# Two of ScalarE's stages change slots: the copy of the first block's transposed attention, and its tiny exponential

## The reference

```
# block 0, channel attention with a squeeze gate
energy = einsum('bcn,bdn->bcd', q, q)                       # q = x as (b, 128, 256)
attention = softmax(max(energy, -1) - energy)
out = einsum('bcd,bdn->bcn', attention, q)
h = relu(concat([x, out], 1).mean((2, 3)) @ w1.T + b1)
se = sigmoid(h @ w2.T + b2)
x = se * x + (1 - se) * out
```

## Time and profile before

| what | value |
|---|---|
| median of 3 runs | 554.14 us |
| lowest and highest | 550.01 and 558.89 us |
| the profiled execution | 552.4 us |
| its span, first to last instruction | 550.6 us |
| granted TensorE clock, mean | 0.922 of 2.4 GHz |
| TensorE busy | 470.5 us, 85% |
| VectorE busy | 348.1 us, 63% |
| ScalarE busy | 262.7 us, 48% |
| GpSimd busy | 134.0 us, 24% |

### The profile page before, as it was taken

How to read it: one execution, slowest core, us unless ns; L and a number is a source line. 1 busy time by engine, 2 the same in 40 slices (tenths; PEclk the granted TensorE clock), 3 DMA queues, 4 the chain that set the end, 5 groups by cost and what they waited for, 6 DMA issues and landing times.

```text
span 550.6 us, 10106 instructions
## 1 busy us (share of the span) xinstructions
PE 470.5 (85%) x3522; PEld 363.9 (66%) x3522; DVE 348.1 (63%) x895; ACT 262.7 (48%) x654; POOL 134.0 (24%) x161
## 2 busy tenths in 40 slices
PE   4286797879998999899889989999998999884995
PEld 3163564556776768676767766676766788784885
DVE  1418844872868577556867775776538343666896
ACT  3332665743554464435454635533444431994541
POOL 5210563242103102110220022111101111512672
PEclk9997786967999999699999989996998899996999
DMA  6000111000000000000000000000000000004112
GB/s 208 19 19 2 43 44 63 0 21 19 2 1 21 20 1 19 19 0 0 19 19 0 0 19 0 0 20 2 1 1 19 2 20 1 2 1 152 40 38 76
DMA packets 9486, 13.15 MB, mean 24 GB/s; under 512 B 496, under 2 KB 8816, under 8 KB 9328
## 3 DMA queue, kind: packets, MB, share of 16 engines
q1 hardware_dynamic: 9456, 12.76, 7.0%
HBM read 8.56 MB, written 4.19 MB: 23 GB/s over the span
## 4 chain that ended last, share of the span: by engine, by line
PE 57%; DVE 17%; ACT 10%; issue 8%; POOL 4%; DMA 4%; DVEq 0%; SPq 0%; ACTq 0%; POOLq 0%
PE bank L1199 7%; PE bank L1201 5%; PE bank L1200 5%; PE bank L1312 5%; PE bank L1394 5%; PE bank L1368 4%; DMA w_stage<-convs 4%; PE bank L1366 2%; PE bank L1344 2%; PE bank L1422 2%; PE bank L1228 2%; ACT x L798 2%; PE bank L1381 2%; ACT prob L740 1%; DVE even L892 1%
## 5 line engine op out<-in xcount | busy, mean ns | idle before, releaser
L1199 PE MATMUL bank<-win,w_hi 128*128 128x256 f32 x384 | 122.3, 318 | 12.3 <-DVE win L1145 5.9
L740 ACT ACTIVATE prob<-bank 128x512 f32<-128x512 f32 x128 | 69.5, 596 | 95.4 <-PE bank L1366 94.7
L1200 PE MATMUL bank<-win,w_hi 128*128 128x256 f32 x384 | 109.4, 285 | 0.0
L1201 PE MATMUL bank<-win,w_lo 128*128 128x256 f32 x384 | 109.3, 285 | 0.0
L992 DVE TENSOR_REDUCE nmax<-bank 128x2 f32<-128x512 f32 x128 | 85.3, 685 | 34.3 <-PE bank L1344 33.9
L1199 PEld LDWEIGHTS bank<-win,w_hi 128*128 128x128 f32 x384 | 74.0, 193 | 23.7 <-issue 10.8
L1200 PEld LDWEIGHTS bank<-win,w_hi 128*128 128x128 f32 x384 | 74.1, 193 | 0.7
L1201 PEld LDWEIGHTS bank<-win,w_lo 128*128 128x128 f32 x384 | 73.7, 192 | 0.0
L517 POOL TENSOR_TENSOR first<-first 128x256 f32<-128x256 f32 x24 | 17.7, 737 | 174.6 <-ACT first L629 174.6
L1368 PE MATMUL bank<-qk 32*128 32x256 f32 x256 | 43.9, 357 | 4.3 <-ACT prob L740 3.8
L1368 PEld LDWEIGHTS bank<-qk 32*128 32x128 f32 x256 | 26.4, 204 | 19.6 <-issue 6.9
(11 more groups left out here) (235 smaller groups left out, 930.4 us busy)
## 6 DMA issues: line engine op xcount, KB each, us to landing
w_stage<-convs SPq DMA_DIRECT2D x4, 576.0 KB, 4.8
x_in<-x SPq DMA_DIRECT2D x8, 256.0 KB, 2.6
out<-x_pair SPq DMA_DIRECT2D x8, 256.0 KB, 2.2
q<-out SPq DMA_DIRECT2D x1, 2048.0 KB, 8.3
out<-v SPq DMA_DIRECT2D x8, 256.0 KB, 2.1
cst<-small SPq DMA_DIRECT2D x1, 1708.0 KB, 9.7
cst<-small SPq DMA_DIRECT2D x1, 253.5 KB, 2.9
```

Of the source, the lines that this page charges most:

```text
L740: act.activation(prob[:, x // 4 % 2, x % 4, :, :], bank[ST_BANK[x % 2]][:, :], ACT.Exp, scale=L2_SCALE).then_inc(st_exp, 1)
L1199: mm(dst, hi, x_hi, start=(row == 0), stop=False)
L1200: mm(dst, hi, x_lo, start=False, stop=False)
L1201: return mm(dst, lo, x_hi, start=False, stop=(row == KH - 1))
```

## The change

Two entries of ScalarE's table get another slot. "att0t" goes from slot 8 to slot 7, and stands there ahead of "ab" in the order of the table; "z0" goes from slot 15 to slot 14. The stages' own code, waits and semaphores stay, as do the tables of the other engines.

```
-ACT_SLOTS = {"xr": 0, "xt": 2, "sum_x": 3, "hid1": 3, "z1": 4, "att0": 6, "ab": 7, "att0t": 8, "o0": 11, "even": 11, "att1": 11,
-             "hid0": 13, "filt": 13, "z0": 15, "red": 19}
+ACT_SLOTS = {"xr": 0, "xt": 2, "sum_x": 3, "hid1": 3, "z1": 4, "att0": 6, "att0t": 7, "ab": 7, "o0": 11, "even": 11, "att1": 11,
+             "hid0": 13, "filt": 13, "z0": 14, "red": 19}
```

## The result

The changed kernel takes 531.33 us (median of 4 runs, 526.66 to 537.17) against 555.03 us for the kernel before (4 runs, 550.01 to 558.89). The ratio is 0.9595, with a 95% interval of 0.9535 to 0.9654: faster by 4.1%. The profiled execution took 526.66 us, span 524.9 us; it is 25.7 us shorter than that of before, and 0.954 of the full clock was granted over its span where before had 0.922.

The account below looks back on a forecast made before the run. TensorE, 57% of the chain of waits, was taken to bind. Copy 7.0, exponential 4.65 and clock 2.3 us sum to 13.95, say 13.9 us: 540.2 us on the median's scale, 2.5% faster; range 533.5 to 548.0 us.

Parts of the forecast that it names:

- The copy, by order of work: ScalarE's copy (line 649) in slot 7 ends TensorE's wait at line 1228: 7.0 us, low end 4.2, high end 8.7.
- new wait at line 1274: At full clock, with the copy's stall gone, TensorE would wait some 0.8 us for VectorE's logits.
- "ab" and GpSimd's sign product have cover: ScalarE's "ab" would start 0.6 us later, but GpSimd's sign product would keep 2.5 us of slack, costing nothing.
- Round 0's 1.0 us: In round 0 GpSimd's sign product ends at 70.16 regardless, so line 1270 moves from 71.22 to about 70.2, 1.0 us.
- The exponential, by order of work: z0 in slot 14 ends TensorE's wait at line 1291 in rounds 1 to 5: 4.65 us, low end 0.
- The sum of the two: A full-clock round, line 1228 to line 1228, shortens from 49.4 us by 1.7 to 47.7 us.
- The clock: TensorE's drops to 1.2 GHz in rounds 0, 3 and 5 may go: 4.6 us, low end 0, half taken, 2.3.
- rival A: The clock gives back all its 4.6 us: 16.2 us in total, 537.9 us; chance 0.20.
- B: VectorE takes the stall back; the copy yields its low end, the clock nothing: 8.9 us, 545.2 us; chance 0.20.
- C: The copy's stall only moves to line 1274 or the next score products; z0 alone pays: 4.65 us, 549.5 us; chance 0.10.
- D: Slower than before, above 554 us: idle time at line 1274 and elsewhere drops the clock in full-clock rounds; chance 0.05.

## Why the prediction was wrong

By its own steps:

- **The copy, by order of work.** Right in mechanism. At full clock I took 0.8 us a round; measured 1.01 (49.41 to 48.40 with the copy alone). In all that is some 5 us and not 7.0: I booked the whole stall, 1.44 and 1.5 us, for the rounds at half clock, but after the change rounds 2 to 5 run at full clock, where a new wait at line 1274 takes part of it back. The new wait at line 1274 was forecast at some 0.8 us and is 0.69 us, VectorE's queue is what makes it, and the 0.28 us at line 1279 went as said. The claim that "ab" and GpSimd's sign product have cover holds, 2.6 us against 2.5. Round 0's 1.0 us did not come, for a load landed later; that it was booked on one profile's date for the load was the mistake.
- **The exponential, by order of work.** Right: 0.93 us forecast and 1.0 us measured, in rounds 1 to 5, with none in round 0.
- **The sum of the two.** 47.7 us was forecast for a round at full clock; it takes 47.4.
- **The clock.** This is the term that failed. I named the mechanism, TensorE falling to 1.2 GHz in the stall, but sized it at 2.3 us with 4.6 us as its most. It is 14.9 us in the rounds of the profile, and 10.7 to 16 us by the two kernels in which the copy's stall, alone or with the other, is filled. Two mistakes made it small. First, I counted only drops that start in the stall itself or within 1 us behind it (rounds 0, 3 and 5; the one of round 3 begins at 222.5, when line 1228 already runs). Round 1's long drop starts earlier, at 113.3, behind a wait of 1.23 us at line 1223, and I let it stand; yet with the copy's stall gone it was shorter, and the round went from 0.88 to 0.97 of the clock, which is worth 6.63 - 2.0 = 4.6 us. I left out the drop in round 6 too, for its round has none of the moved stages. It cost 4.3 us all the same: from line 1291 of round 5 to that of round 6 before takes 50.27 us and the changed kernel 46.00. Second, I halved the term because a shorter stall remains at line 1274, and put its low end at 0 because rounds 2 and 4 had the same stall and no drop. The remaining stall, 0.69 us, brought no drop in rounds 2 to 5 of the changed kernel. And rounds 2 and 4 say that a stall doesn't bring a drop each time, not that a drop seen had another cause; the kernels with the copy's stall filled show no drop in rounds 2 to 5 at all.
- **The rule of the Trainium skill** (TensorE: Matmul & The Clock Gate, "A second HAM failure mode: psum-queue depth-cycling"), that short idle times between groups of matmuls, coming often enough, make the clock swing, was the better guide, and even rival A, built on it, was priced too low. The filled kernels agree with it: ratio 0.9712 with the idle time filled, and no drop from 117 to 372 us. They also show its limit here: filling the 0.93 us stall alone gave 0.9985.
- **The rivals.** B and C fall: the copy's stall came back at line 1274 by under half. D falls, for the clock rose. A had the right direction, but not the price: it gave 537.9 us, and the measured time is 6.6 us below it.

What stays open is round 6. A drop stands there in the kernel before and in those with one part alone (the last stretch has 0.90, and 0.94 in each of the two), and is missing in the changed kernel, with both stalls filled and with the copy's filled. But the changed kernel with products at the end has it again, as the only one of the seven profiles in which both stages are moved. So it isn't settled whether its absence is the change's doing. It is 4.3 us of the 14.9.

## What to carry to other kernels

A stall of TensorE is worth its own length and, where the trace shows the granted clock falling in rounds that hold it, the time at half clock as well; here the second was the larger of the two. Price it with every drop in the rounds that contain such a stall, not with those alone that begin in it, and test it by filling the stall with unused products: this changes no dependence between the stages and splits the two terms in one run. A drop in a part that another engine paces costs next to nothing, as in the last convolutions here. Filling pays where the wait is certain and the clock still full; products that ran at half clock outlasted the wait here (6.98 us against 5.86).

## What the runs showed of the hardware that I had not expected

The kernel before does 3% better (0.9712, 0.9654 to 0.977) when TensorE does 28 more products (56 matmul instructions) in an execution, whose results nobody reads. The effect was uneven: a stall of 1.45 us in six rounds cost 10.7 us through the clock, and one of 0.93 us in five rounds cost nothing that could be measured while the first was there.
